# A depthwise convolution moved from VectorE to TensorE inside a Mamba scan stage, with a new share of weighing

## The reference

```python
h = (x - mu) * lax.rsqrt(var + LN_EPS) * ln_g + ln_b
xz = jnp.einsum('bld,de->ble', h, W_in)
u, z = jnp.split(xz, 2, axis=-1)
u_t = jnp.transpose(u, (0, 2, 1))
u_t = lax.conv_general_dilated(u_t, conv_w, window_strides=(1,), padding=[(D_CONV - 1, 0)],
                               feature_group_count=D_INNER, dimension_numbers=('NCH', 'OIH', 'NCH'))
u_t = u_t + conv_b[None, :, None]
u = jax.nn.silu(jnp.transpose(u_t, (0, 2, 1)))
x_dbl = jnp.einsum('bld,de->ble', u, W_xproj)
dt, Bm, Cm = jnp.split(x_dbl, [DT_RANK, DT_RANK + D_STATE], axis=-1)
dt = jax.nn.softplus(jnp.einsum('blr,rd->bld', dt, W_dt) + b_dt)
dA = jnp.exp(jnp.einsum('bld,dn->bldn', dt, A))
dBu = jnp.einsum('bld,bln->bldn', dt * u, Bm)
# scan over time: hc = dA_t * hc + dBu_t;  y_t = sum over n of hc * C_t
y = jnp.transpose(ys, (1, 0, 2)) + u * D
y = y * jax.nn.silu(z)
out = jnp.einsum('bld,dm->blm', y, W_out)
return x + out
```

## Time and profile before

| what | value |
|---|---|
| median of 3 runs | 4958.69 us (4956.91 to 4969.4) |
| the profiled execution | 4959.75 us, its span 4958.0 us |
| busy over the span | PE 79%, POOL 50%, DVE 57%, ACT 45% |
| first scan starts, last scan ends | 61.06 us, 992.91 us |
| stage of the change | about the first 1000 us of 4958 |

### The profile page before, as it was taken

How to read it: one execution, slowest core, us unless ns; L and a number is a source line. 1 busy time by engine, 2 the same in 40 slices (tenths; PEclk the granted TensorE clock), 3 DMA queues, 4 the chain that set the end, 5 groups by cost and what they waited for, 6 DMA issues and landing times.

```text
span 4958.0 us, 49367 instructions
## 1 busy us (share of the span) xinstructions
PE 3917.7 (79%) x15216; PEld 2269.9 (46%) x15218; DVE 2847.6 (57%) x4916; ACT 2214.3 (45%) x4082; POOL 2468.8 (50%) x2152
## 2 busy tenths in 40 slices
PE   6888888759957888797677869994884698888892
PEld 2333333347734556576333336663572233334571
DVE  5999999951136665211688862226433676764522
ACT  5565656421136775111555533333243455555241
POOL 5999999922212234211789854442355422222256
PEclk8999999959978889898788879995996699998896
DMA  5556556522210010321455531115155422221145
GB/s 152 157 162 159 157 157 163 145 77 85 83 54 17 18 35 26 102 87 62 132 159 145 145 106 45 45 42 159 36 160 121 127 41 40 43 37 55 39 141 132
DMA packets 312121, 476.73 MB, mean 96 GB/s; under 512 B 34890, under 2 KB 167990, under 8 KB 311786
## 3 DMA queue, kind: packets, MB, share of 16 engines
q1 hardware_dynamic: 277152, 388.87, 28.6%
q0 software_dynamic: 29184, 76.12, 5.5%
q10 hardware_dynamic: 5504, 8.39, 0.6%
HBM read 375.26 MB, written 97.49 MB: 95 GB/s over the span
## 4 chain that ended last, share of the span: by engine, by line
PE 37%; POOL 6%; DVE 5%; issue 4%; DMA 4%; ACT 3%; SPq 0%; DVEq 0%; ACTq 0%; POOLq 0%
PE s_gate_up L2325 8%; PE s_result_sum L2341 4%; PE s_hidden_sum L1761 3%; PE s_result_sum L1772 3%; PE s_out_sum L3696 3%; POOL s_h L435 2%; PE s_shared L2981 2%; PE s_scores L3637 2%; DVE s_maxima L3328 2%; PE s_scores_T L3680 2%; PE s_shared L2991 1%; POOL s_gathered L1047 1%; POOL s_h L444 1%; PE s_transposed L2315 1%; PE s_mid_transposed L2334 1%
## 5 line engine op out<-in xcount | busy, mean ns | idle before, releaser
L435 POOL TENSOR_TENSOR s_h<-s_dtu,s_bc 128x1024 f32<-128x1024 f32 x384 | 902.3, 2357 | 71.7 <-PE s_y_sum L477 56.1
L477 PE MATMUL s_y_sum<-s_h,identity 128*128 128x512 f32 x1536 | 776.6, 644 | 145.6 <-POOL s_h L444 132.1
L402 ACT ACTIVATE s_decay<-s_dt,s_A 128x512 f32<-128x512 f32 x768 | 498.5, 682 | 333.3 <-DVE s_h L377 326.5
L477 PEld LDWEIGHTS s_y_sum<-s_h,identity 128*128 128x128 f32 x1536 | 296.8, 203 | 586.9 <-issue 312.5
L2325 PE MATMUL s_gate_up<-s_w_gate_up,s_rowsT 128*128 x1184 | 420.2, 487 | 2.1 <-issue 1.9
L3502 ACT ACTIVATE s_weights_T<-s_scores_T 128x1024 f32<-128x1024 f32 (+3 forms) x384 | 292.6, 811 | 256.4 <-PE s_scores_T L3680 254.8
L3328 DVE TENSOR_REDUCE s_maxima<-s_scores 128x1 f32<-128x512 f32 (+3 forms) x463 | 296.7, 659 | 178.2 <-PE s_scores L3641 96.7
L444 POOL TENSOR_TENSOR s_h<-s_h,s_bc 128x512 f32<-128x512 f32 x288 | 365.8, 1271 | 27.8 <-DVE s_h L370 19.4
L2384 DVE TENSOR_TENSOR s_mid<-s_act,s_gate_up 128x128 f32<-128x128 f32 (+1 forms) x228 | 92.8, 407 | 451.0 <-ACT s_act L2357 451.0
L3550 POOL TENSOR_SCALAR_AFFINE_SELECT s_weights_T<-s_weights_T 128x256 f32<-128x256 f32 x256 | 102.7, 406 | 468.6 <-ACT s_weights_T L3502 465.9
L370 DVE TENSOR_TENSOR_SCAN s_decay<-s_decay,s_carry,s_h 128x512 f32<-128x512 f32 x240 | 305.4, 1288 | 24.8 <-POOL s_clip_flag L2653 11.2
(11 more groups left out here) (533 smaller groups left out, 7690.6 us busy)
## 6 DMA issues: line engine op xcount, KB each, us to landing
s_bc<-s_bc_rows SPq DMA_DIRECT2D x384, 512.0 KB, 5.2
sorted_results<-s_result SPq DMA_DIRECT2D x160, 128.0 KB, 2.2
s_w_inter<-in_L_ffn_experts_inter SPq DMA_DIRECT2D x16, 1024.0 KB, 5.0
s_w_exp_out<-in_L_ffn_experts_out SPq DMA_DIRECT2D x16, 1024.0 KB, 8.3
s_queries<-parts_of_q SPq DMA_DIRECT2D x96, 128.0 KB, 4.6
s_keys<-parts_of_k SPq DMA_DIRECT2D x96, 128.0 KB, 7.5
results_by_token<-zeros SPq DMA_DIRECT2D x16, 512.0 KB, 5.8
s_pair<-results_by_token SPq DMA_DIRECT2D x16, 512.0 KB
```

Source lines behind the costliest of these rows:

```text
L402: S.e.activation(self.decay[:, (2 * g + d) % 4, :], dt[q // self.passes % 2][:, at, :], ACT.Exp, scale=A[:, at, g % ns:g % ns + 1]).then_i ...
L435: G.e.tensor_tensor(self.h[r][:], dtu[q // self.passes % 2][:, at:at + 2, :], mid(self.bc[r][:, 0, :], 2), ALU.mult).then_inc(*self.fed.up())
L477: made = T.e.matmul(self.y[:, d, :], ident[:], self.h[r][:, d, :], start=False, stop=g % ns == ns - 1)
```

## The change

The taps of the convolution become four TensorE products for each channel block: a tile `taps` holds for each block and tap a 128x128 diagonal matrix (identity times the tap's weights, built once by GpSimd in four instructions of 128x512 at the start of the stage), and the moving operand is a view of the input, shifted by 0 to 3 columns. So that the views can reach back, the input is copied by ScalarE into a tile `xb` of 3+512 columns for each block, the first three being the end of the chunk before (or zeros). Two blocks are copied at once. The four products of a block add up in the same PSUM bank, which ScalarE then reads into `u` with the bias. VectorE's taps, its saved columns and GpSimd's late terms go. ScalarE's four instructions of 128x512 (L629 before) become four of the same size (the sums) and two copies of 128x1024, and one small one for the history columns. The shares become (1, 1, 2, 1, 2, 1, 1, 2): VectorE weighs 11 tiles in 8 units and GpSimd 5.

```diff
-    sc = Scan(K, M, PASSES, NS, (1, 1, 1, 2), prologue=58)
+    sc = Scan(K, M, PASSES, NS, (1, 1, 2, 1, 2, 1, 1, 2), prologue=58)
...
-    cv = M.sb("conv", [P, ND, CH])
+    xb = M.sb("conv_in", [P, ND, 3 + CH])
+    taps = M.sb("conv_taps", [P, ND, 4, P])
...
-            for d, tick in enumerate((23, 26, 30, 33)):
-                taken = bank[:, d % 2, :]
-                yield tick
-                V.wait_ge(*tap_begun.at(ND * c + d))
-                if c % CPB != CPB - 1:
-                    V.wait_ge(*late_made.at(c // CPB - 1))
-                    V.e.tensor_copy(hist[:, d, :], taken[:, CH - 3:CH]).then_inc(*hist_made.up())
-                for t in (2, 1, 0):
-                    o = 3 - t
-                    V.e.scalar_tensor_tensor(cv[:, d, o:CH], taken[:, 0:CH - o], vec[:, d, t:t + 1], cv[:, d, o:CH],
-                                             ALU.mult, ALU.add).then_inc(*(tapped if t == 0 else step).up())
-                    if t:
-                        yield tick + o
-                        V.wait_ge(*step.now())
...
-            for d, tick in enumerate((20, 21, 28, 31)):
-                yield tick
-                S.wait_ge(*in_made.at(8 * c + d))
-                S.wait_ge(*u_made.at(c - 1))
-                S.e.activation(cv[:, d, :], bank[:, d % 2, :], ACT.Identity, bias=vec[:, d, 4:5], scale=vec[:, d, 3:4]).then_inc(
-                    *tap_begun.up())
+            for h, (copy, sums) in enumerate(((20, (23, 25)), (28, (31, 33)))):
+                yield copy
+                if h == 0:
+                    S.wait_ge(*tapped.at(ND * c - 1))
+                    before = xb[:, :, CH:CH + 3] if c % CPB else K.zeros[:, 0:3 * ND].rearrange("p (d t) -> p d t", d=ND)
+                    S.e.activation(xb[:, :, 0:3], before, ACT.Copy).then_inc(*begun.up())
+                S.wait_ge(*in_made.at(8 * c + 2 * h + 1))
+                S.wait_ge(*begun.at(c))
+                S.e.activation(xb[:, 2 * h:2 * h + 2, 3:], bank[:], ACT.Copy).then_inc(*x_copied.up())
+                for d, tick in zip((2 * h, 2 * h + 1), sums):
+                    yield tick
+                    S.wait_ge(*tapped.at(ND * c + d))
+                    S.wait_ge(*out_made.at(c - 2))
+                    S.e.activation(u[r][:, d, :], bank[:, d % 2, :], ACT.Identity, bias=vec[:, d, 4:5]).then_inc(*summed_up.up())
...
+            def tap(d, tick):
+                for j in range(0, 4, 2):
+                    yield tick + j // 2
+                    if j == 0:
+                        T.wait_ge(*x_copied.at(2 * c + d // 2))
+                        T.wait_ge(*taps_made.at(0))
+                    for i in (j, j + 1):
+                        made = T.e.matmul(bank[:, d % 2, :], taps[:, d, i, :], xb[:, d, i:i + CH], start=i == 0, stop=i == 3)
+                made.then_inc(*tapped.up())
+                free[d % 2] = summed_up.at(ND * c + d)
...
-            for s, tick in enumerate((18, 19, 27, 30, 34, 36, 40, 41)):
+            for s, tick in enumerate((18, 19, 25, 26, 34, 36, 40, 41)):
...
+                if s in (1, 3):
+                    yield from tap(s - 1, tick + 2 if s == 1 else tick + 3)
+                    yield from tap(s, tick + 4 if s == 1 else tick + 5)
```

More of the change, by code:

```diff
@@ L512, in mamba_stage @@
     hT = M.sb("hT", [P, DT, CH])
-    cv = M.sb("conv", [P, ND, CH])
+    xb = M.sb("conv_in", [P, ND, 3 + CH])
+    taps = M.sb("conv_taps", [P, ND, 4, P])
     soft = M.sb("softplus", [P, 2, CH])
-    hist = M.sb("conv_history", [P, ND, 3])
-    late_x = M.sb("conv_late", [P, ND, 3])
-    late_t = M.sb("conv_late_term", [P, ND, 3])
     zs, u, dt, dtu = ([M.sb(f"{n}{i}", [P, ND, CH]) for i in range(2)] for n in ("z", "u", "dt", "dtu"))
@@ L520, in mamba_stage @@
     vec_here, w_in_here, w_here, a_exp, a_ready = *K.events(3, 16, "dma"), *K.events(2)
-    step, step_g, normed, turned, h_made, in_made, tap_begun, tapped, hist_made = K.events(9)
-    z_copied, late_made, late_added, u_made, z_made, bc_made, rows_made, dtp_made = K.events(8)
+    normed, turned, h_made, in_made, taps_made, begun, x_copied, tapped, summed_up = K.events(9)
+    z_copied, u_made, z_made, bc_made, rows_made, dtp_made = K.events(6)
     abs_made, soft_exp, log_made, dt_made, dtu_made, out_made, out_added = K.events(7)
@@ L635, in front @@
             yield 43
-            S.wait_ge(*tapped.at(ND * c + ND - 1))
-            if c % CPB:
-                S.wait_ge(*late_added.at(c // CPB))
-            S.wait_ge(*out_made.at(c - 2))
-            S.e.activation(u[r][:], cv[:], ACT.Silu).then_inc(*u_made.up())
+            S.wait_ge(*summed_up.at(ND * c + ND - 1))
+            S.e.activation(u[r][:], u[r][:], ACT.Silu).then_inc(*u_made.up())
             S.wait_ge(*z_copied.at(c))
@@ L668, in gpsimd @@
     def gpsimd():
-        def then(inst):
-            inst.then_inc(*step_g.up())
-            G.wait_ge(*step_g.now())
         def early(c):
@@ L677, in front @@
         def front(c):
-            yield 37
-            if c % CPB:
-                G.wait_ge(*hist_made.at(ND * (c // CPB) + ND - 1))
-                G.wait_ge(*late_added.at(c // CPB - 1))
-                then(G.e.tensor_tensor(late_x[:], hist[:], last(vec[:, :, 0], 3), ALU.mult))
-                for t in (1, 2):
-                    n = 3 - t
-                    then(G.e.tensor_tensor(late_t[:, :, 0:n], hist[:, :, t:3], last(vec[:, :, t], n), ALU.mult))
-                    add = G.e.tensor_tensor(late_x[:, :, 0:n], late_x[:, :, 0:n], late_t[:, :, 0:n], ALU.add)
-                    if t == 1:
-                        then(add)
-                add.then_inc(*late_made.up())
-                G.wait_ge(*tapped.at(ND * c + ND - 1))
-                G.wait_ge(*late_made.at(c // CPB))
-                G.e.tensor_tensor(cv[:, :, 0:3], cv[:, :, 0:3], late_x[:], ALU.add).then_inc(*late_added.up())
             yield 57
@@ L707, in gpsimd @@
         G.wait_ge(*vec_here.now())
+        G.wait_ge(*K.ident_here.at(0))
+        for d in range(ND):
+            made = G.e.tensor_tensor(taps[:, d, :, :], mid(K.ident[:], 4), last(vec[:, d, 0:4], P), ALU.mult)
+        made.then_inc(*taps_made.up())
         sc.gpsimd(dtu, dtu_made, early=early, front=front, late=late)
@@ L734, in front @@
                 made.then_inc(*in_made.up())
-                free[s % 2] = tapped.at(ND * c + s) if s < ND else z_copied.at(c) if s < ND + 2 else z_made.at(2 * c + 1)
+                if s in (1, 3):
+                    yield from tap(s - 1, tick + 2 if s == 1 else tick + 3)
+                    yield from tap(s, tick + 4 if s == 1 else tick + 5)
+                if s < ND:
+                    continue
+                free[s % 2] = z_copied.at(c) if s < ND + 2 else z_made.at(2 * c + 1)
             yield 46
```

## The result

| what | before | after |
|---|---|---|
| median (range) | 4959.36 us (4956.91 to 4969.4, 4 runs) | 5028.32 us (5016.4 to 5037.83, 4 runs) |
| ratio, with its 95% interval | | 1.0134 [1.0118, 1.0150] |
| the profiled execution | 4959.75 us, span 4958.0 | 5037.83 us, span 5036.1 |
| first scan starts, last scan ends | 61.06, 992.91 us | 73.3, 1065.4 us |

A forecast was written before the change was run, and what follows sets the result against it. The prediction took VectorE to set the pace of the scan. Weighings 18.6, burst 21.8 and prologue 13.6 us gave +54 on the profiled 4959.75, 5014, so 5013 by the median; own range 4992 to 5030, overall 4972 to 5045.

The forecast's parts named there:

- The bound: First stage's scan: VectorE sets the pace, so relieving GpSimd gains nothing; each added weighing costs 0.58 us.
- D: Variant within the forecast: weighings hide in VectorE's waits for ScalarE (4995), or diagonals cost the upper price (5018).
- The burst: Units 11 to 17: 36 TensorE products of 0.86 us make VectorE wait about 11 us per chunk, +21.8 us.
- Rival A: Units 11 to 17: TensorE keeps up, the stretch takes 23.0 us, 4931 in all; chance 0.12.
- B: Units 11 to 17: VectorE's wait is 7.7 us shorter in each of seven chunks, 4959; chance 0.07.
- The prologue: Before the first scan: copies and taps on the path 12.4 us, diagonals 1.2, together +13.6 us.
- the step that counts the new shares at 18.6 us: Whole scan: 32 more weighings on VectorE at 0.58 us each; GpSimd's saved 39 us counts nothing.
- Rival C: Units 11 to 17: TensorE at the 1.2 GHz level loses 4 us in each of seven chunks, 5042; chance 0.18.

The follow-up runs named there:

- experiments 8 and 10: Kernel before plus six spare TensorE products at ticks 58 to 63: with the new shares 4971.63 us, with the old shares 4961.99 us.
- experiment 2: Kernel before with the new shares alone, the taps still on VectorE: 4994.13 us, 1.0054.
- experiment 3: Changed kernel with two of the four tap products of each block left out, so the output lacks them: 4970.53 us, 1.0024.
- experiment 4: Changed kernel with the second pass's `take_y` two units later, in unit 19 in place of 17: 5033.4 us, 1.0129.
- experiment 1: Changed kernel with the old shares (1, 1, 1, 2), the taps staying on TensorE: 4999.94 us, 1.0069.
- experiment 7: Changed kernel with six spare, unread TensorE products at the end of chunks 0 to 6: 5008.19 us, 1.0089.
- experiment 11: Kernel before with blocks 0 and 1 on TensorE except in the first chunk, old shares, plus six spare products at ticks 58 to 63: 4958.53 us, 0.9993.

## Why the prediction was right or wrong

**The bound: right.** VectorE set the pace, and each weighing cost its start-to-start time: 18.4 us for 32, of 18.6, and 18.5 between experiments 8 and 10. Relieving GpSimd brought nothing: 39 us of its work went, and its idle time ahead of the feeds, waiting for TensorE's sums, grew instead:

```profile
L435 POOL TENSOR_TENSOR s_h<-s_dtu,s_bc 128x1024 f32<-128x1024 f32 x256 | 608.4, 2388 | 136.8 <-PE s_y_sum L477 127.5 <-issue 5.2 <-ACT s_carry L414 3.1
```

The groups view of GpSimd shows 136.8 us of idle time ahead of the feeds (before it was 26.3). D, that the weighings hide in ScalarE's waits, fell: these waits grew after, and with the new shares alone they stayed (29.1 us in experiment 2).

**The burst: right.** Start 2.7 us in, 36 products at 0.86, `take_y` and unit 18 at 35.4 in chunks 1, 3 and 5, all as worked out; experiment 3 supports the unit price from the other side (6.5 us for eight products, 6.9 by the count). Two things are off in size. W17 is 9.6 to 10.0, not some 11, because VectorE was held up ahead of it, 1.4 to 3.1 us by ScalarE's decays and 0.5 by a feed; the end is the same. And chunks 2 and 6 took 36.5 and 36.2. There the low level had come back ahead of the stretch, after a wait for `s_hT`, so the projection was late, and the first tap started 3.9 us into the stretch (874.72 less 870.8 in chunk 6), 1.2 later than in chunk 3:

```profile
866.93 3.66 PE L718 MATMUL s_front<-s_hT,s_w_in 128*128 128x512 f32 x4 [2.93 <-ACT s_hT L607]
```

With 0.2 us more in each of chunks 0 and 4 that is the 2.6 us over the forecast's 21.8. Rival A needed products at 0.6 us, and fell. B's escape, an order that lets unit 15 past, was tried in its nearest form in experiment 4: moving the reader gave 10 us at most.

**The prologue: nearly right**, 12.2 of 13.6. z was copied at 48.76, 12.5 us later than in the earlier trace rows: 0.5 from the diagonals (1.2 forecast) and 12.0 from copies and taps (12.4 forecast):

```profile
25.39 1.03 ACT L617 ACTIVATE s_conv_in<-s_front 128x1024 f32<-128x1024 f32 x1 [5.86 <-PE s_front L718]
...
37.08 1.03 ACT L617 ACTIVATE s_conv_in<-s_front 128x1024 f32<-128x1024 f32 x1 [2.74 <-PE s_front L718]
...
48.76 1.02 ACT L626 ACTIVATE s_z<-s_front 128x1024 f32<-128x1024 f32 x1 [2.74 <-PE s_front L718]
```

The diagonals took GpSimd until 10.69, and the factors began at 10.78, where they had at 10.26:

```profile
6.66 4.03 POOL L680 TENSOR_TENSOR s_conv_taps<-identity,s_mamba_vectors 128x512 f32<-128x512 f32 x4 [6.16 <-DMA s_A<-in_L_attn_a_A_log]
```

Four instructions took 4.03 us, 1.01 each. The 1.23 came from the scan's product of the same size; that is the mis-sized term.

**What failed: the step that counts the new shares at 18.6 us.** It weighed them by VectorE's instructions alone and put their effect on TensorE at nothing. With them the 1.2 GHz level at the chunk's end lasted longer, just ahead of unit 1's `take_y`, which waited 18.3 us more in the profiled execution. By medians it is 28 less 18.6, some 9 us, from experiment 1, 32 less 18.6, some 14, from experiment 2, and up to the 20 us that the spare products win back in experiment 7. Rival C had the right mechanism in the wrong place: it put the low level into the burst, where the granted clock was 1.00, and priced it at 28. The time alone doesn't decide between the two: 5028 is 15 us over the forecast and 14 under C's 5042, and it lies only 2 us inside the forecast's own range. That it lies inside is in part luck; the seven waits of 9.6 to 10.0 us and the granted clock in the stretches decide for the forecast's mechanism. The profiled execution is 24.1 us over the forecast's 54: this term 18.3, the burst 2.6, the prologue -1.4, the weighings -0.2, the rest 4.8, of which 5.6 lie in unchanged stages. It is the slowest of four; their median is 15 us over the forecast.

What stays open: why the new shares lengthen the low level. Before, the gap and the low level are there in the same place too, and the level ends a few products sooner:

```profile
410.97 6.84 PE L477 MATMUL s_y_sum<-s_h,identity 128*128 128x512 f32 x8 [2.85 <-POOL s_h L444]
417.74 1.98 PE L752 MATMUL s_front<-s_rows,s_w_dt 17*128 17x512 f32 x4
```

Its gap, 2.85 us, is no shorter than those after (2.46, 2.24), so longer gaps are not the explanation. A gap of 2.23 us was followed by 13 us of the low level or by none at two boundaries of experiment 2. Which of the pattern's weighings decides it was not tried.

## What to carry to other kernels

When work moves to an engine that has idle time, count that engine's instructions from the point where they can first start to the one that someone waits for, at their start-to-start distance, and compare the end with the reader's time: the share of idle time says nothing. Moving the reader later helps little when a ring passes the delay on; a smaller share of the work does (half the blocks, with the first chunk left on VectorE, the old shares, moved ticks and spare products, won 0.5%, where all of them with the new shares lost 1.3%). And after a change of shares compare the granted clock and the waits just ahead of each product that is waited for: here the shares alone moved them.

## What the runs showed of the hardware

- The 1.2 GHz level came after gaps of 1.0 to 2.5 us between short runs of products, for 13 us (granted clock 0.50); after a like row of gaps (1.48, 0.84, 2.23) it did not come at all. In the kernel after, 42 unused products of 0.86 us made the runs 20 us faster (5028.3 to 5008.2) and four times closer (21 to 5 us, four runs each); in experiment 11 two spells of some 3 us stayed.
- How long it lasts differs by chunk and, as the spread of the runs suggests, also by execution: W1 was 0, 0.3, 3.2, 4.2, 4.4, 5.1 and 5.9 us in seven chunks of one execution. A change of this size wants more than one profile.
- Float32 products of 128x512 with a moving operand shifted by 0 to 3 columns cost what aligned ones do, 0.86 us.
